# A graph network's attention sweep: node work cut into pieces between groups, two node one-hot buffers, no filling matmuls

## The chip, the core and the metric

The program runs on one core of one Trainium2 chip, as one launch. The metric is the device time of that launch in microseconds. The engines are named as the profile names them: PE (TensorE; PEld is its weight load), DVE (VectorE), ACT (ScalarE), POOL (GpSimd) and SP (SyncE). Each runs its own list of instructions in order, and they wait for each other through semaphores.

## The reference

Four graph layers, each added to its input and normalised over the 64 features, over 12,500 nodes and 200,000 edges (sorted by destination). The change touches only the first, an attention layer with four heads:

```python
h = (x @ W).reshape(N, H, D)
a_src = jnp.einsum('nhd,hd->nh', h, att_src)
a_dst = jnp.einsum('nhd,hd->nh', h, att_dst)
alpha = leaky_relu(a_src[src] + a_dst[dst], 0.2)
alpha = jnp.exp(alpha - amax[dst])
denom = segment_sum(alpha, dst)
msg = h[src] * (alpha / denom[dst])[:, :, None]
out = segment_sum(msg, dst).reshape(N, H * D) + bias
x = layernorm(x + out @ Wl + bl)
```

## The kernel before

Seven passes go over the graph: `gat` (this layer), then `dev`, `gine` and four `sage` passes. The change is in `gat`, which takes about microseconds 180 to 2990 of the profile; then a table of edge counts is built and the other passes use it.

**Tiling.** The 200,000 edges, ordered by destination, are cut into 392 groups of 512 (4 columns of 128). The 12,500 nodes are 98 tiles of 128, and 7 tiles are a block, so there are 14 blocks. Destinations are skewed: the first block takes 14 rounds of 8 groups (112 groups), the last a single round. A group whose edges end in one tile and begin in the next has a further tile ("second tile" in the code) and needs its one-hot and its sum twice.

**One group.** SP loads the edges' indices and a copy of their destinations. POOL gathers the sources' rows with four indirect DMAs (L671) into one of 8 slots, so it can be up to some groups ahead. DVE makes a node one-hot (L1683, nodes by edges, for each tile of the group), and PE multiplies it with the nodes' scores (`expand`, 12 narrow matmuls of L879 per tile, opened by L872 and closed by L883), which gives every edge its destination's score. DVE adds the scores (L1701 to L1706, `logit_ready`), ACT takes the exponent (L1127) and issues the load of the edges' features (L1130, `edges_loaded`), and then makes the one-hot of edges by nodes (L1135, L1138). DVE multiplies rows by weights (L1712, `messages_ready`), PE sums messages per node (`aggregate`: L833 narrow, then L844, 8 wide f32 matmuls), and DVE adds the sum to the block's accumulator (L1650). A further tile's one-hot is L1644 on DVE.

**Order.** The code is written out by hand. PE does `expand(g + 1)` ahead of `aggregate(g)`; DVE makes the node one-hot of group g + 1 inside group g. There is one buffer `nodehot`, so the second one-hot of a group waits (`expand_done`) until PE has read the first. Ahead of `logit_ready`, ahead of every `nodehot_ready` and ahead of `messages_ready`, PE multiplies zeros with zeros (`fill`, L817): 5, 5 per tile, and 6 matmuls of 128 columns.

**End of a block.** DVE normalises the block's sums (`gat_normalise`, L1294, L1439 to L1447), PE transposes them (`node_tensor`, L729, 14 matmuls), ACT copies the transposed sums to SBUF (L1212). Their product with the folded output weights (`gat_product`, L770, 28 matmuls), the residual sum, the layer norm (L1346 to L1326, with a square root on ACT, L1166) and the cutting into three bf16 parts (L1294, L1355, L1333 on DVE; L1183 and three DMAs on ACT) are the late half. It is done one block later, ahead of that block's own transposes: `late_half`, with `b - 1`. At the end of the last block both late halves remain, one ahead of its transposes and one behind them:

```python
def dense(b, late=None):       # PE
    if late:
        late()                 # gat_product(b - 1)
    node_tensor(pe, k, b)
    pe.wait_ge(step_sem["copied"], ...)
```

PE enters the next block's rounds only when the copy has ended.

## Time and profile before

| what | us |
|---|---|
| median of 3 runs | 10120.04 |
| lowest and highest | 10109.03 and 10133.09 |
| span of the profiled execution | 10126.3 |
| PE, DVE, POOL and ACT busy in it | 6982.7, 4777.3, 4577.3, 1864.3 |

The page gives the profiled execution's span, and no separate time of that execution; the span is within 6.3 us of the median of the runs. The busy shares (69%, 47%, 45%, 18%) are over seven passes with different limits, so they say little on `gat`. The stretch to read is that of the sweep, cut at the ends of blocks: a block ends where ACT copies (L1212), and the first instruction of each group on DVE is L1701. The timeline's "idle before" names what ended the wait; "issue" means nothing that the profile shows.

### The profile page before, as it was taken

What the parts mean: (1) busy time and instruction counts of PE and PEld (TensorE: products, weight loads), DVE (VectorE), ACT (ScalarE), POOL (GpSimd) and SP (SyncE); (2) the same over time, 40 slices, a digit from 0 to 9 for tenths busy, and PEclk for the clock granted to TensorE, in tenths of its full rate; (3) what the DMA queues carried; (4) which work ended last, traced back from release to release, by engine and by line L of the source; (5) the groups of instructions that cost most, each with busy time, mean ns of one, the idle gap of its engine ahead of it and who ended that gap; (6) DMA issues with size and microseconds to landing.
All of it is one profiled execution on the core that took longest, in us unless ns stands there. A gap on an engine that the chain in (4) does not pass through costs nothing.

```text
span 10126.3 us, 269255 instructions
## 1 busy us (share of the span) xinstructions
PE 6982.7 (69%) x70494; PEld 5130.6 (51%) x70495; DVE 4777.3 (47%) x12912; ACT 1864.3 (18%) x3800; POOL 4577.3 (45%) x4467
## 2 busy tenths in 40 slices
PE   5888777787754666666777876675777455565677
PEld 4666656565541222112454545665676454454676
DVE  4555555554458877776444333333332332333344
ACT  2333333332220234553000000000000000000000
POOL 3777665554420000001763017442653765763764
PEclk9898888888877888999888987887888677777788
DMA  2444333333320112234555566665676677677676
GB/s 64 95 95 91 88 83 89 83 79 74 72 69 13 63 78 111 127 128 167 164 174 183 177 211 194 213 213 184 215 237 213 201 275 265 207 254 240 205 261 233
DMA packets 973408, 1566.58 MB, mean 155 GB/s; under 512 B 499841, under 2 KB 621441, under 8 KB 966402
## 3 DMA queue, kind: packets, MB, share of 16 engines
q1 hardware_dynamic: 485762, 1244.14, 35.5%
q0 software_dynamic: 150016, 196.43, 9.4%
q10 hardware_dynamic: 337280, 122.87, 4.7%
q14 instruction: 317, 2.60, 0.1%
q8 instruction: 33, 0.54, 0.0%
HBM read 1337.91 MB, written 225.00 MB: 154 GB/s over the span
## 4 chain that ended last, share of the span: by engine, by line
PE 36%; issue 21%; DVE 16%; DVEq 11%; POOL 10%; DMA 5%; ACT 1%; ACTq 0%; SPq 0%; POOLq 0%
PE ps_turn L997 15%; POOL ARENA L671 10%; PE ps_out L844 6%; PE ps_turn L952 4%; PE ps_pair L844 2%; DMA ARENA<-edge_attr 2%; DVE ARENA L1834 2%; DVE ARENA L1836 2%; PE ps_turn L817 2%; DMA ARENA<-counts 2%; DVEq L1841 1%; PE ps_pair L1019 1%; DVEq L466 1%; PE ps_pair L879 1%; DVE ARENA L1924 1%
## 5 line engine op out<-in xcount | busy, mean ns | idle before, releaser
L997 PE MATMUL ps_turn<-ARENA 128*128 128x192 bf16 (+2 forms) x28812 | 2789.3, 266 | 760.6 <-DVE DSUM L1987 347.0
L997 PEld LDWEIGHTS ps_turn<-ARENA 128*128 128x128 bf16 x28812 | 2353.9, 108 | 1206.1 <-issue 901.0
L671 POOL DMA_INDIRECT ARENA<-table_sage,idx x1920 | 1876.0, 977 | 1330.9 <-issue 985.7
L671 POOL DMA_INDIRECT ARENA<-table_gat,idx x1568 | 1740.9, 1110 | 1044.4 <-DMA idx<-src_r 537.1
L952 PE MATMUL ps_turn<-ARENA 128*128 128x392 bf16 (+1 forms) x4204 | 1064.6, 359 | 673.7 <-DVE ARENA L1836 376.5
L671 POOL DMA_INDIRECT ARENA<-table_dev,idx x480 | 473.2, 986 | 1665.2 <-ACT idx L1220 1520.6
L1834 DVE TENSOR_SCALAR ARENA<-ARENA 128x784 bf16<-128x784 f16 (+1 forms) x2102 | 1008.6, 480 | 358.4 <-issue 229.0
L952 PEld LDWEIGHTS ps_turn<-ARENA 128*128 128x128 bf16 (+1 forms) x4204 | 334.3, 101 | 1403.7 <-issue 1359.6
L671 POOL DMA_INDIRECT ARENA<-table_gine,idx x480 | 468.4, 976 | 908.0 <-issue 687.5
L1202 ACT ACTIVATE ARENA<-ps_turn 128x784 f32 x784 | 645.3, 823 | 1081.7 <-PE ps_turn L952 1080.9
L1987 DVE TENSOR_REDUCE DSUM<-ps_turn 128x64 f32<-128x192 f32 (+2 forms) x686 | 263.6, 384 | 1137.5 <-PE ps_turn L997 975.5
L817 PE MATMUL ps_turn<-ZEROS 128*128 128x128 bf16 x6762 | 571.3, 226 | 239.7 <-issue 185.3
L1914 DVE SCALAR_TENSOR_TENSOR ARENA<-DST,TBASE,COL 128x512 f32 x720 | 493.6, 747 | 512.8 <-issue 512.8
L817 PEld LDWEIGHTS ps_turn<-ZEROS 128*128 128x128 bf16 x6762 | 436.6, 101 | 375.0 <-issue 338.1
L1019 PE MATMUL ps_pair<-ARENA 128*128 128x64 bf16 (+2 forms) x8640 | 388.2, 209 | 313.2 <-DMA ARENA<-table_sage,idx 161.4
L844 PE MATMUL ps_out<-ARENA 128*128 128x320 f32 x1568 | 565.6, 513 | 0.0
L1220 ACT ACTIVATE idx<-ARENA 128x16 int32 x192 | 40.7, 215 | 2778.6 <-PE ps_turn L1041 2693.4
L1135 ACT ACTIVATE tmp<-COL,dst_in 128x128 bf16<-128x128 f32 x1568 | 501.1, 390 | 253.7 <-issue 253.7
L1019 PEld LDWEIGHTS ps_pair<-ARENA 128*128 128x128 bf16 x8640 | 363.6, 108 | 335.7 <-issue 333.0
L1836 DVE TENSOR_SCALAR ARENA<-ARENA 128x128 bf16<-128x128 f16 (+1 forms) x2102 | 521.3, 248 | 0.0
L844 PE MATMUL ps_pair<-ARENA 128*128 128x320 f32 x1568 | 509.0, 471 | 0.0
L1034 PE MATMUL ps_out<-ARENA,more_hots 128*128 128x64 bf16 (+2 forms) x3528 | 227.4, 216 | 388.5 <-issue 217.6
(303 smaller groups left out, 6737.4 us busy)
## 6 DMA issues: line engine op xcount, KB each, us to landing
ARENA<-counts SPq DMA_DIRECT2D x1764, 448.0 KB
counts<-ARENA SPq DMA_DIRECT2D x49, 3136.0 KB, 9.0
ARENA<-counts SPq DMA_DIRECT2D x588, 224.0 KB
ARENA<-dst_b SPq DMA_DIRECT2D x393, 256.0 KB
ARENA<-edge_attr ACTq DMA_DIRECT2D x392, 128.0 KB
ARENA<-table_sage,idx POOLq DMA_INDIRECT x1920
ARENA<-table_gat,idx POOLq DMA_INDIRECT x1568
nodes_dev<-table_rows ACTq DMA_DIRECT2D x14, 672.0 KB
```

The costliest lines, as they stand in the source:

```text
L671: pool.indirect_dma_start(ps["buf"][:, s, c, 0:ps["row"]], None, ps["table"][:, :], bass.IndirectOffsetOnAxis(idx[:, s, c:c + 1], 0)).then ...
L817: pe.matmul(ps_fill, ZERO[:, :], ZERO[:, :], start=True, stop=True)
L844: last = pe.matmul(sums[:, 0:MSGW if gat else n], lhs, rhs, start=(c == 0 and q == 0), stop=(c == C - 1 and q == parts - 1))
L952: last = pe.matmul(ps_turn[:, at:at + WIDE_ROW // 2], marks[:, 0:P], marks[:, P + q * (WIDE_ROW // 2):P + (q + 1) * (WIDE_ROW // 2)], star ...
L997: last = pe.matmul(ps_dense[half][:, 0:n], RING[:, b, :], XP[:, b, :], start=(b == PIECE_AT[pieces[0]]), stop=(j == pieces[-1] and b == PI ...
L1019: last = pe.matmul(ps_pair[:, (4 * h + q) * P:(4 * h + q) * P + n], tile_hots[:, ((4 * h + q) * C + c) * P:((4 * h + q) * C + c + 1) * P], ...
L1135: act.activation(distance[:, c * P:(c + 1) * P], COL[:, :], ACT.Abs, scale=-1.0, bias=dst_in[:, s % 2, c:c + 1]).then_inc(hot_distance, 1)
L1202: act.activation(to[:, :, c * CHUNK:(c + 1) * CHUNK].rearrange("p (q b) v -> p q b v", q=2), sums.rearrange("p q (b v) -> p q b v", v=CHUN ...
L1834: ve.tensor_scalar(marks[:, P:P + WIDE_ROW], IOTA16, BASES[:, bass.ds(q, 1)], KEY_pad[:, bass.ds(j, 1)], ALU.add, ALU.is_equal).then_inc(r ...
L1836: ve.tensor_scalar(marks[:, 0:P], COL16, AKEY_pad[:, bass.ds(j, 1)], None, ALU.is_equal).then_inc(ready, 1)
L1914: return ve.scalar_tensor_tensor(ring.rearrange("p (c v) -> p c v", c=C), DST[:, bass.ds(cols, C)].unsqueeze(2).broadcast_to([P, C, P]), T ...
L1987: ve.tensor_reduce(DSUM[:, half, 0:n], ps_dense[half][:, 0:3 * n].rearrange("p (q v) -> p v q", q=3), X_AXIS, ALU.add).then_inc(dense_read, 1)
```

## The change

Four things are changed, all in `gat`.

1. The late half of block b is cut into pieces, and the pieces stand between the groups of the first round of block b + 1: `gat_product` on PE in `expand` of group slot 2, the head (residual sum, mean, variance) on DVE behind slot 3, the square root on ACT behind slot 4, the tail (scale, cut) on DVE behind slot 5, the rows' copies and DMAs on ACT behind slot 7. A phase register per engine says whether a piece is due; every round tests it, and a round that has none due branches past it. A second copy of each piece stands ahead of `gat_normalise`, for a block that has no round.
2. `nodehots` has two buffers, and `expand_done` starts at 2.
3. The filling matmuls of zeros are gone.
4. At a block's end PE waits only for the copy of the last 256 columns (`end_copied`), which now comes first; the load of the old rows is issued behind the copies, into `big`.

```diff
-        nodehot = gat_area(GE // 2, dt=BF16)
+        nodehots = gat_area(GE, dt=BF16)
...
-        old_x = gat_area(TB * D).rearrange("p (t d) -> p t d", t=TB)
...
+        old_x = big[:, 0:TB * D].rearrange("p (t d) -> p t d", t=TB)
...
-        def sweep(eng, one_round, finish, dense, late=None):
+        def sweep(eng, phase, one_round, finish, dense, pieces):
+            eng.reg_mov(phase[0], NO_PHASE)
+            eng.reg_mov(phase[2], 0)
             with eng.Fori(0, BLOCKS) as b:
                 r0 = eng.value_load(SCHED[0:1, bass.ds(b, 1)], min_val=0, max_val=ROUNDS)
                 r1 = eng.value_load(SCHED[0:1, bass.ds(b + 1, 1)], min_val=0, max_val=ROUNDS)
@@ -504,16 +504,19 @@
                 last_block = eng.value_load(SCHED[0:1, BLOCKS + 1:BLOCKS + 2], min_val=0, max_val=BLOCKS)
                 with eng.If(last_block.eq(b)):
                     finish()
-                if late is None:
-                    dense(b)
-                else:
-                    dense(b, lambda: late_half(eng, b, late))
-            if late is not None:
-                late(BLOCKS - 1)
-        def late_half(eng, b, late):
-            with eng.If(b > 0):
-                late(nc.s_assert_within(b - 1, 0, BLOCKS - 1, skip_runtime_bounds_check_because="b > 0"))
+                for j, piece in enumerate(pieces):
+                    piece_here(eng, phase, j, piece)
+                dense(b)
+                eng.reg_mov(phase[0], 0)
+                eng.reg_mov(phase[2], b)
+            for piece in pieces:
+                piece(BLOCKS - 1)
+        def piece_here(eng, phase, j, piece):
+            with at_phase(eng, phase, j):
+                piece(eng.snap(phase[2], min_val=0, max_val=BLOCKS - 1))
+                eng.reg_add(phase[0], phase[0], 1)
...
-            def fill(n):
-                for _ in range(n):
-                    pe.matmul(ps_fill, ZERO[:, :], ZERO[:, :], start=True, stop=True)
...
-                def expand(g, lo, hi):
-                    fill(5)
+                def expand(g, lo, hi, product=False):
                     pe.wait_ge(logit_ready, g + 1)
+                    if product:
+                        settle(pe)
+                        piece_here(pe, gat_phase, 0, lambda b: gat_product(pe, b))
                     pe.matmul(ps_exp_all[:, 0:C * 2 * H], ZERO[:, :], ZERO[:, 0:C * 2 * H], start=True, stop=False)
                     with pe.Fori(lo, hi) as t:
                         pe.reg_add(spread, spread, 1)
-                        fill(5)
                         pe.wait_ge(nodehot_ready, pe.snap(spread, min_val=1, max_val=GROUPS * TILES))
+                        hot = nodehots[:, bass.ds(pe.snap(spread_at, min_val=0, max_val=GE), GE)]
                         for c in range(C):
                             for q in range(3):
-                                last = pe.matmul(ps_exp[:, c, :], nodehot[:, c * P:(c + 1) * P],
+                                last = pe.matmul(ps_exp[:, c, :], hot[:, c * P:(c + 1) * P],
                                                  VALS[:, bass.ds(t, 1), q, :].rearrange("p a k -> p (a k)"),
                                                  start=False, stop=False)
                         last.then_inc(expand_done, 1)
+                        pe.reg_alu(spread_at, spread_at, GE, ALU.bitwise_xor)
...
-                            expand(g + 1, *next_span(pe, spans, s))
+                            expand(g + 1, *next_span(pe, spans, s), s == 2)
...
-                            fill(6)
...
-                def dense(b, late=None):
-                    if late:
-                        late()
+                def dense(b):
                     node_tensor(pe, k, b)
-                    if gat:
-                        pe.wait_ge(step_sem["copied"], block_count("copied", "gat", b))
-                        settle(pe)
+                    pe.wait_ge(end_copied, b + 1)
+                    settle(pe)
...
+                    if s == 4:
+                        piece_here(act, gat_phase, 0, lambda b: node_root(0, b, b))
+                    if s == 7:
+                        piece_here(act, gat_phase, 1, lambda b: node_rows(0, b, b))
...
-            def gat_copy(b, late):
-                late()
+            def gat_copy(b):
                 act.wait_ge(step_sem["turned"], block_count("turned", "gat", b))
                 act.wait_ge(product_read, b + 1)
                 settle(act)
+                act.activation(bigT[:, 1536:TB * H * D], ps_turn[:, 1536:TB * H * D], ACT.Copy).then_inc(end_copied, 1)
+                act.activation(bigT[:, 0:1536], ps_turn[:, 0:1536], ACT.Copy).then_inc(step_sem["copied"], 1)
                 act.dma_start(old_x, x.rearrange("(t p) d -> p t d", p=P)[:, bass.ds(b * TB, TB), :]).then_inc(old_x_loaded, 16)
-                act.activation(bigT[:, :], ps_turn[:, 0:TB * H * D], ACT.Copy).then_inc(step_sem["copied"], 1)
...
-                xb = a[:, :, 0:D]
-                ve.wait_ge(step_sem["product"], block_count("product", ps["name"], b))
-                ve.wait_ge(old_x_loaded, b * 16 + 16)
-                step(ve.tensor_tensor(y, view(ps_gat, D), old_x, ALU.add))
-                ve.sem_inc(product_read, 1)
-                step(ve.tensor_tensor(y, y, row(CV[:, :]), ALU.add))
-                layer_norm(b, y, xb)
-                both = view(big, 2 * D)
-                if not isinstance(b, int):
-                    ve.wait_ge(step_sem["turned"], block_count("turned", "gat", b) + 1)
-                    settle(ve)
-                step(same(both[:, :, 0:D], xb))
-                step(ve.tensor_tensor(both[:, :, D:2 * D], xb, xb, ALU.mult))
-                store_parts(2 * D)
+                xb, y = a[:, :, 0:D], view(tmp[:, 2, :], D)
+                if head:
+                    ve.wait_ge(step_sem["product"], block_count("product", ps["name"], b))
+                    ve.wait_ge(old_x_loaded, b * 16 + 16)
+                    step(ve.tensor_tensor(y, view(ps_gat, D), old_x, ALU.add))
+                    ve.sem_inc(product_read, 1)
+                    step(ve.tensor_tensor(y, y, row(CV[:, :]), ALU.add))
+                    centre(b, y)
+                if tail:
+                    scale(b, y, xb)
+                    both = view(big, 2 * D)
+                    step(same(both[:, :, 0:D], xb))
+                    step(ve.tensor_tensor(both[:, :, D:2 * D], xb, xb, ALU.mult))
+                    store_parts(2 * D)
...
-            ve.wait_ge(rows_free, b + 1)
+            ve.wait_ge(rows_free, b + 2)
...
+                        if s == 3:
+                            ve.wait_ge(expand_open, g + 2)
+                            settle(ve)
+                            piece_here(ve, gat_phase, 0, lambda b: late(b, True))
+                        if s == 5:
+                            piece_here(ve, gat_phase, 1, lambda b: late(b, False))
```

How the instruction lists move. TensorE, slot 1 of a round, the expansion of the next group. Before:

```order
L817 MATMUL ps_turn<-ZEROS 128x128 x5
L871 REGISTER_ALU
L872 MATMUL ps_pair<-ZEROS 128x32 [waits logit_ready]
L873 UNCONDITIONAL_BRANCH
L873 ISA
L817 MATMUL ps_turn<-ZEROS 128x128 x5
L879 ISA [waits nodehot_ready]
L879 MATMUL ps_pair<-ARENA 128x8
L879 ISA
L879 MATMUL ps_pair<-ARENA 128x8
L879 ISA
L879 MATMUL ps_pair<-ARENA 128x8 x10
```

TensorE, the same place in the changed kernel:

```order
L873 MATMUL ps_pair<-ZEROS 128x32 [waits logit_ready]
L874 UNCONDITIONAL_BRANCH
L874 ISA
L877 ISA [waits nodehot_ready]
L880 ISA
L880 MATMUL ps_pair<-ARENA 128x8
L880 ISA
L880 MATMUL ps_pair<-ARENA 128x8
L880 ISA
L880 MATMUL ps_pair<-ARENA 128x8
L880 ISA
L880 MATMUL ps_pair<-ARENA 128x8 x3
```

The zeros (`ps_turn<-ZEROS`) are gone, and because the one-hot's address is now in a register, more register instructions (`ISA`) stand between the narrow matmuls.

ScalarE, from the one-hot of slot 4 to the exponent of slot 5. Before:

```order
L1138 ACTIVATE ARENA<-tmp,ONE 128x512 [waits hot_distance]
L1126 REGISTER_ALU
L1127 ACTIVATE ARENA<-ARENA 128x4x4 [waits logit_ready]
L1130 ISA
L1130 DMA ARENA<-edge_attr 128x4x64
```

ScalarE, the same place in the changed kernel:

```order
L1136 ACTIVATE ARENA<-tmp,ONE 128x512 [waits hot_distance]
L457 REGISTER_ALU
L458 COMPARE_AND_BRANCH
L518 ISA
L1166 ACT_TABLE_LOAD
L1166 ACTIVATE small<-small 128x7 [waits var_ready]
L519 REGISTER_ALU
L517 UNCONDITIONAL_BRANCH
L1124 REGISTER_ALU
L1125 ACT_TABLE_LOAD
L1125 ACTIVATE ARENA<-ARENA 128x4x4 [waits logit_ready]
```

The square root with its table load is branched past where it isn't due, but the second table load, ahead of the exponent, stands outside the branch and is done in every round.

VectorE, the beginning of the late half's head. Before, behind the normalising of a block's sums (`big<-ARENA,small`):

```order
L1447 TENSOR_TENSOR big<-ARENA,small 128x1792
L78 REGISTER_ALU
L515 COMPARE_AND_BRANCH [waits vector_step]
L1345 ISA [waits product]
L1346 TENSOR_TENSOR tmp<-ps_pair,ARENA 128x448 [waits old_x_loaded]
L78 ISA
L1348 TENSOR_TENSOR tmp<-tmp,CV 128x448 [waits vector_late_step]
```

VectorE in the changed kernel, behind slot 3 of a round (`L1742` is the last of that slot):

```order
L1742 REGISTER_ALU
L457 REGISTER_ALU [waits expand_open]
L458 COMPARE_AND_BRANCH
L518 ISA
L1364 ISA [waits product]
L1365 TENSOR_TENSOR tmp<-ps_pair,big 128x448 [waits old_x_loaded]
L78 ISA
L1367 TENSOR_TENSOR tmp<-tmp,CV 128x448 [waits vector_late_step]
```

The head now stands between two groups, behind a wait for the next group's expansion that every round makes.

## Rows read from the trace of the kernel before

**Rows 1.** Stretches; per engine busy us (x instructions), then TensorE's granted clock, DMA share.
```profile
...
core 0: us, PE busy (x) PEld busy (x) DVE busy (x) ACT busy (x) POOL busy (x), PEclk, DMA share, GB/s
190.00:827.00 637.00, 539.98 (x5848) 404.19 (x5847) 339.73 (x1024) 248.89 (x667) 499.85 (x451) 0.90 0.43 95
...
827.00:2980.00 2153.00, 1664.44 (x17822) 1257.43 (x17822) 1093.01 (x3059) 712.68 (x1772) 1204.85 (x1104) 0.87 0.36 81
...
```

**Rows 2.** Waits of POOL from 180 to 827: releaser, total us, times, longest us.
```profile
...
POOL ARENA L671 <- issue: 137.5, 451, 0.3
...
```

**Rows 3.** Waits of POOL from 827 to 2980.
```profile
...
POOL ARENA L671 <- DMA idx<-src_r: 536.2, 119, 32.9
...
```

**Rows 4.** The stretch 827 to 2980, line 1701 alone (one instruction per group).
```profile
...
827.00:2980.00 2153.00, 48.10 (x280) 0.87 0.36 81
...
```

**Rows 5.** The stretch 827 to 2980, line 1644 alone (one per further tile).
```profile
...
827.00:2980.00 2153.00, 66.89 (x89) 0.87 0.36 81
...
```

**Rows 6.** Timeline, end of block 0: start us, duration us, engine, work, idle before.
```profile
...
810.30 0.17 DVE L1701 TENSOR_TENSOR ARENA<-ps_pair,ARENA 128x16 f32<-128x16 f32 x1
...
828.26 0.17 DVE L1701 TENSOR_TENSOR ARENA<-ps_pair,ARENA 128x16 f32<-128x16 f32 x1 [7.91 <-issue]
...
```

**Rows 7.** Timeline, end of block 1, DVE, PE and ACT.
```profile
...
1055.94 0.17 DVE L1701 TENSOR_TENSOR ARENA<-ps_pair,ARENA 128x16 f32<-128x16 f32 x1 [0.39 <-PE ps_pair L883]
...
1066.37 3.38 PE L770 MATMUL ps_pair<-MST,bigT 128*128 128x64 f32 x28
...
1069.89 0.62 DVE L1346 TENSOR_TENSOR tmp<-ps_pair,ARENA 128x448 f32<-128x448 f32 x1 [2.31 <-PE ps_pair L770]
...
1078.16 1.09 DVE L1333 TENSOR_TENSOR tmp<-big 128x896 f32<-128x896 f32 x1
...
1085.40 1.28 ACT L1212 ACT_TABLE_LOAD   x1 [2.54 <-issue]
...
1088.95 0.17 DVE L1701 TENSOR_TENSOR ARENA<-ps_pair,ARENA 128x16 f32<-128x16 f32 x1 [9.71 <-issue]
...
```

**Rows 8.** Timeline, end of block 12.
```profile
...
2869.88 0.17 DVE L1701 TENSOR_TENSOR ARENA<-ps_pair,ARENA 128x16 f32<-128x16 f32 x1 [0.92 <-DVE ARENA L1650]
...
2898.96 0.17 DVE L1701 TENSOR_TENSOR ARENA<-ps_pair,ARENA 128x16 f32<-128x16 f32 x1 [9.65 <-issue]
...
```

**Rows 9.** Waits of DVE from 827 to 2980.
```profile
...
DVE ARENA L1683 <- PE ps_pair L879: 259.7, 84, 7.3
...
```

**Rows 10.** Timeline, a group with one tile behind another.
```profile
...
1047.69 0.17 DVE L1701 TENSOR_TENSOR ARENA<-ps_pair,ARENA 128x16 f32<-128x16 f32 x1 [0.91 <-PE ps_pair L883]
...
1052.19 0.45 PE L833 MATMUL ps_pair<-ARENA 128*128 128x5 bf16 x12 [0.74 <-DMA ARENA<-edge_attr]
...
1052.49 2.40 PE L844 MATMUL ps_pair<-ARENA 128*128 128x320 f32 x8
...
1054.73 0.44 PE L817 MATMUL ps_turn<-ZEROS 128*128 128x128 bf16 x5
...
1055.31 0.45 PE L879 MATMUL ps_pair<-ARENA 128*128 x12
...
1056.41 0.45 PE L833 MATMUL ps_out<-ARENA 128*128 128x5 bf16 x12 [0.26 <-issue]
...
```

**Rows 11.** Timeline, a node one-hot pair between two sums.
```profile
...
2514.43 2.40 PE L844 MATMUL ps_out<-ARENA,tmp 128*128 128x320 f32 x8
...
2517.84 0.49 DVE L1683 TENSOR_SCALAR ARENA<-ARENA,NODE 128x512 bf16<-128x512 int32 x1 [7.00 <-PE ps_pair L879]
...
2518.48 0.65 PE L879 MATMUL ps_pair<-ARENA 128*128 x12 [0.48 <-DVE ARENA L1683]
...
2519.93 0.44 PE L833 MATMUL ps_pair<-ARENA 128*128 128x5 bf16 x12
...
```

**Rows 12.** Timeline, one group's sum some microseconds earlier.
```profile
...
2510.20 4.09 PE L844 MATMUL ps_out<-ARENA 128*128 128x320 f32 x8
...
```

**Rows 13.** Waits of ACT from 827 to 2980.
```profile
...
ACT ARENA L1127 <- DVE ARENA L1706: 987.9, 278, 15.3
...
```

More of the change, by code:

```diff
@@ L1313, in layer_norm, with centre @@
             def layer_norm(b, y, dst):
-                mean, var, std = small[:, 0, 0:TB], small[:, 1, 0:TB], small[:, 2, 0:TB]
+                centre(b, y)
+                scale(b, y, dst)
+            def centre(b, y):
+                mean, var = small[:, 0, 0:TB], small[:, 1, 0:TB]
                 sq = view(tmp[:, 3, :], D)
```

58 lines of the change are left out of this document (34 added, 24 removed).

## The prediction

> **What bounds the kernel now.** I read the page's slices first, then the same counts cut at the ends of blocks, then the waits of POOL, DVE and ACT in the two stretches that this shows, and then the timelines of one group, one pair of one-hots and one block's end. The sweep has two regimes. Up to 827 us (block 0, 112 groups) POOL is the bound: its gathers are busy for 499.85 of 637 us [rows 1], and between them it only pays its own issue time, 137.5 us over 451 gathers, with no wait for a slot worth naming [rows 2]. A gather costs 1.4 us there, so a group 5.6 us, whatever PE and DVE do. From 827 to 2980 us (blocks 1 to 13) POOL is busy for 1204.85 of 2153 us [rows 1] and waits 536.2 us for indices [rows 3], whose load waits for a free slot: the consumers, PE, DVE and ACT, are the bound. That stretch holds 280 groups [rows 4] in 35 rounds, and 89 further tiles [rows 5], so 369 sums on PE. Only there can the change win. What POOL would need for the 1104 gathers at block 0's price is 1104 x 1.4 = 1546 us, so up to 607 us of the stretch are open, and POOL doesn't cut the forecast below. What comes behind the sweep is the same code and is left at its time.
>
> **Term 1, the ends of blocks.** The end of block 0 has no late half in it: from the last group's first DVE instruction to the next block's it takes 828.26 - 810.30 = 18.0 us [rows 6]. The end of block 1 has one and takes 1088.95 - 1055.94 = 33.0 us [rows 7]; the twelfth after it, of block 12, takes 2898.96 - 2869.88 = 29.1 us [rows 8]. I take the mean of these two of twelve, 31.1. The difference of 13.1 us is DVE's half (1069.89 to 1079.25), PE's product of 3.38 us ahead of the transposes, and ACT's copies behind them [rows 7]. It leaves the end. At 18 us the end is set by DVE's way into the next block (7.9 us of idle behind the normalising, [rows 6]), so the copy's order (256 columns first) gives nothing more; the table load of 1.28 us [rows 7] now starts only when the transposes are done, but still ends in that cover. DVE, PE and ACT gain two branches each: I take 0.5 us. 13 x (13.1 - 0.5) = 164 us less, the thirteenth being the one behind the last block, of the same kind.
>
> **Term 2, the same work between groups.** It isn't gone. PE's 3.4 us go between two groups; DVE's head (five instructions of 0.62 us, some small ones) is 4.4 us, its tail 4.6 us. The wait for `expand_open` at slot 3 queues nothing that would not have waited for it at slot 4. Behind the head on DVE stands the next group's L1701, and PE waits for it with the expansion after next; meanwhile PE has one sum of 2.40 us [rows 10] to do. Bounds: 0, if the slack of PE and DVE takes it all, and 3.4 + 4.4 + 4.6 = 12.4 us, if none. PE is nearly full in this stretch (1664.44 of 2153 us, [rows 1]), so I take no cover for its part, and about 40% for DVE's: 8.5 us. 13 x 8.5 = 110 us more. ACT's part (square root, three copies, DMAs) stands behind slots 4 and 7; ACT waits 987.9 us for 278 exponents in this stretch [rows 13], 3.6 us each, and slot 7 is followed by DVE's own way round the loop: nothing.
>
> **Term 3, the second one-hot.** With one buffer DVE stands 259.7 us in 84 waits for PE to read the first one-hot [rows 9]. PE pays too: in [rows 11] its sum ends at 2516.83 and the next begins at 2519.93, a gap of 3.10 us. In it are 21 filling matmuls and 0.48 us of waiting for the second one-hot. In the group with one tile the gap is 1056.41 - 1054.89 = 1.52 us [rows 10]. With two buffers DVE makes both one-hots and the messages long before PE has finished its sum; what stays is two expansions of 0.45 us, opening and closing, about 1.1 us. So PE gains 2.0 us of a gap of 3.1; DVE's 259.7 / 84 = 3.1 us is the other end. I take 2.3: 89 x 2.3 = 205 us less (bounds 1.0, the fills of one such gap alone, and 3.1).
>
> **Term 4, the fills in groups with one tile.** Five fills show as 0.44 us [rows 10]; the 16 hold PE, pipelined, for about 1.1 of the 1.52 us. But the group has another chain: from L1701 (1047.69) over the exponent and the load of the edges' features to the sum that waits for that load (1052.19) it is 4.50 us [rows 10]. L1701 of group g + 1 waits for an expansion that PE does behind the sum of g - 1, so two groups cost at least 4.50 + 2.7 (the sum) + 0.9 (the expansion) = 8.1 us, 4.05 each. The group of [rows 10] takes 1056.41 - 1052.19 = 4.22 us. The gain is then 0.17 there, more where PE runs at half clock and the fills cost double. Bounds 0 and 1.1; I take 0.35, near the row: 191 x 0.35 = 67 us less. In block 0 it gives nothing, POOL covers it.
>
> **Term 5, the clock.** The granted clock is 0.87 in the stretch [rows 1]; with its two levels of 1.2 and 2.4 GHz that is 26% of the time at 1.2. A sum takes 2.40 us at the upper [rows 10] and 4.09 at the lower [rows 12], 1.7 more. The fills are part of what keeps PE busy, and DVE, PE and the edge load now leave gaps in their place, so the clock must fall somewhat. Against a collapse speaks rows 11 and 12 together: the sum at 2510.20 ran at the lower clock, was itself 4.09 us of unbroken matmuls, and the sum at 2514.43 was back at 2.40. A slow sum fills PE and brings the clock back. I take a clock of 0.80, 40% at the lower level: 369 x 0.14 x 1.7 = 88 us more. Bounds: 0, and all at the lower level, 369 x 0.74 x 1.7 = 464.
>
> The Trainium skill, "TensorE: Matmul & The Clock Gate", section "Part 1: The HAM clock gate (the "warmup" mystery)", says that the engine is throttled by default and that activity releases the throttle, and its table "Why this matters for your kernels" asks to keep TensorE busy. That speaks against this edit. The trace agrees on the direction (rows 11 and 12); if the rule were followed to its end the sum would be that of rival B.
>
> **Term 6, small things in every round.** Three engines test the phase and branch; ACT loads a table of 1.28 us [rows 7] ahead of slot 5's exponent, mostly inside its 3.6 us of waiting [rows 13]. 0.7 us x 35 = 25 us more (bounds 0 and 2). The register instructions between the narrow matmuls: the 12 matmuls of a first tile take 0.45 us and those of the second, with two such instructions visible, 0.65 [rows 10, 11]; six more would be 0.6 us where PE has just been released, and nothing where its sequencer is ahead during a sum. 0.1 x 369 = 37 us more (bounds 0 and 0.6 each, 220).
>
> **Sum.** -164 + 110 - 205 - 67 + 88 + 25 + 37 = -176 us. The profiled span was 10126.3, which gives 9950. That span is 6 us above the median of the runs, less than I can resolve, so 9950 is the forecast for the median as well.
>
> **Rivals.**
> A: the moved work is hidden and the clock holds. Terms 2 and 5 near zero: 10126 - 176 - 110 - 88 = 9750. For it: DVE is busy for only 1093 of 2153 us [rows 1], and POOL shows that the slots are full at the ends. Against it: the chain of a group passes DVE four times, so its idle time isn't free time, and PE has 23% left.
> B: slower, by the clock. Without fills PE stays at 1.2 GHz for most of the sweep. Terms as above with 464 in place of 88: 10126 - 176 + 376 = 10326; block 0 would add some, since a group at that clock takes 4.09 + 0.45 + about 1.1 = 5.6 us, just POOL's 5.6. It decides from where term 5 eats the other terms' 264 us: 264 / (369 x 1.7) = 0.42 more of the time, 68% at the lower level, a mean clock of 0.66. For it: the fills are 16 of a group's matmul instructions of full width, and there are gaps of idle at every block's end. Against it: rows 11 and 12.
> C: the work only changes its place. The pieces cost their full 12.4 us (term 2: 161), the one-hot pair gives 1.0 (term 3: 89): 10126 - 164 + 161 - 89 - 67 + 88 + 25 + 37 = 10117, no change. For it: nothing of the late half is removed. Against it: 259.7 us of DVE's waits have one cause that is removed.
>
> **How the numbers follow.** The forecast's own case, 9850 to 10040, has 66%; A 12%; C, with times from 10040 to 10146, 12%; B 10%. About 0.2%, 20 us, is what a measurement of this kernel tells from no change. Of C, half is faster by more than that. Faster: 0.66 + 0.12 + 0.05 = 0.83; the same 0.06; slower 0.11. The range 9820 to 10100 holds the forecast's case, half of A and half of C, and leaves B out.
>
> **What would show it.** Right: in the windows of block 0 no change and POOL still without waits for slots; DVE's waits for its node one-hot gone; ends of blocks of 18 to 19 us; the pieces' instructions in the first round of each block, with that round 8 us longer; a granted clock of about 0.80 in blocks 1 to 13; L833 waiting more often for the edges' load; POOL's waits for indices down from 536 to some 360 us. Wrong: a clock under 0.66 (B); rounds with pieces over 12 us longer (C); block 0 longer than 640 us, which would mean that PE at the lower clock has become slower than POOL.

## The result: 10060.1 us, 0.6% faster; the forecast was 9950

The changed kernel takes 10060.12 us (median of 4 runs, 10058.58 to 10074.73), the kernel before 10123.38 in the same session (4 runs). The ratio is 0.9938, 95% interval 0.9921 to 0.9955: 63 us less, where 173 were forecast. The profiled span went from 10126.3 to 10057.1 us.

I cut both traces by the start of the first VectorE instruction of every group (L1701 before, L1722 after; there are 392). The rows of this table are sums of such differences; "later pass" runs from the 181st to the 321st reduction of a step sum, in code that the change doesn't touch.

| us of the profiled execution | before | after | difference |
|---|---|---|---|
| block 0, 112 groups | 625.1 | 630.8 | +5.7 |
| its end | 18.0 | 19.1 | +1.1 |
| ends of blocks 1 to 12 | 375.5 | 229.2 | -146.3 |
| first round (8 groups) of blocks 1 to 12 | 668.5 | 820.3 | +151.8 |
| their other 22 rounds | 1026.7 | 1004.6 | -22.1 |
| block 13 | 53.4 | 60.8 | +7.4 |
| from its last group to the build | 52.0 | 40.9 | -11.1 |
| the later pass | 1322.4 | 1269.6 | -52.8 |
| all the rest | 5984.6 | 5981.7 | -2.9 |

So the sweep, which was to give everything, gave about 14 us, and 53 came from a pass with the same code as before. The ends of blocks are as forecast. The first rounds took back more than the ends gave.

The windows of the changed kernel, cut as those of [rows 1]; the columns are busy us by engine with instruction counts, then PE's clock:

```profile
182.00:831.00 649.00, 494.85 (x4058) 338.05 (x4058) 342.07 (x1037) 269.17 (x689) 504.17 (x465) 0.82 0.45 95
831.00:2974.00 2143.00, 1560.99 (x12930) 1095.77 (x12930) 1109.58 (x3065) 759.02 (x1820) 1189.49 (x1093) 0.79 0.36 81
```

The clock fell from 0.87 to 0.79, as term 5 had it (0.80). The waits of POOL, DVE and PE in the second of these windows (what waited, for what, us in total, times, longest):

```profile
POOL ARENA L674 <- DMA idx<-src_r: 538.5, 147, 16.3
...
DVE ARENA L1722 <- issue: 340.3, 122, 8.3
DVE ARENA L1669 <- PE ps_out L843: 303.5, 165, 3.3
DVE ARENA L1702 <- issue: 147.3, 246, 0.8
DVE ARENA L1722 <- PE ps_pair L885: 71.9, 62, 3.7
...
PE ps_out L832 <- DVE tmp L1663: 130.1, 26, 8.1
PE ps_pair L873 <- DVE ARENA L1727: 124.7, 36, 6.7
```

POOL waits for indices as long as in [rows 3], 538.5 against 536.2 us, so the consumers are not faster. DVE's 259.7 us of [rows 9], waiting for the node one-hot, are gone; L1669, the addition of a group's sums, now waits 303.5 us for PE (168.0 before, in the window of [rows 9]). ACT waits 1044 us for DVE to finish the scores it takes the exponent of, 988 in [rows 13].

One piece, in the first round of block 4 (start us, duration, what, and in brackets the idle time before it):

```profile
1563.16 0.48 DVE L1669 TENSOR_TENSOR ARENA<-ARENA,ps_out 128x325 f32 x1
1564.82 0.62 DVE L1365 TENSOR_TENSOR tmp<-ps_pair,big 128x448 f32<-128x448 f32 x1 [1.18 <-PE ps_pair L885]
1565.13 2.40 PE L843 MATMUL ps_pair<-ARENA 128*128 128x320 f32 x8
...
1565.59 0.62 DVE L1367 TENSOR_TENSOR tmp<-tmp,CV 128x448 f32<-128x448 f32 x1
...
1569.08 0.17 DVE L1337 TENSOR_SCALAR small<-small 128x7 f32<-128x7 f32 x1
...
1570.89 0.17 DVE L1722 TENSOR_TENSOR ARENA<-ps_pair,ARENA 128x16 f32<-128x16 f32 x1 [1.64 <-issue]
```

The head takes 1564.82 to 1569.25. PE's sum is over at 1567.5, 3.4 us before the next group's scores (L1722) can begin. PE has no work in between: the piece is the chain. It also waits 1.18 us for the expansion, whose last matmul began at 1564.04; PE had done the product from 1555.54 to 1558.85 and had no pause over 0.7 us from there on. That the product is what made the expansion late is likely by this, not shown. Behind the head, 1.07 of DVE's 1.64 us of idle time are the load of the next groups' spans into registers, which stands at slots 0 and 4 of every round.

### The profile page after: what moved, and what is told of

Same layout as the page of the kernel before. It is cut to its first block, busy times and chain, and to the rows that moved or that the text cites. A ratio compares the mean times of both kernels' runs of the same rounds, so it can differ in the third digit from the quotient of the medians.

```text
span 10057.1 us, 259505 instructions
## 1 busy us (share of the span) xinstructions
PE 6810.5 (68%) x63732; PEld 4878.1 (49%) x63733; DVE 4790.5 (48%) x12912; ACT 1926.9 (19%) x3863; POOL 4569.1 (45%) x4467
## 4 chain that ended last, share of the span: by engine, by line
PE 34%; issue 21%; DVE 18%; DVEq 12%; POOL 7%; DMA 7%; ACT 1%; SPq 0%; ACTq 0%; POOLq 0%
PE ps_turn L994 14%; PE ps_out L843 8%; POOL ARENA L674 7%; DMA ARENA<-edge_attr 4%; PE ps_turn L949 3%; DVE ARENA L1859 3%; DVE ARENA L1861 2%; DMA ARENA<-counts 2%; PE ps_pair L843 2%; DVEq L425 1%; PE ps_pair L1016 1%; DVEq L466 1%; DVEq L1859 1%; PE ps_out L832 1%; PE ps_out L1031 1%
## 5 line engine op out<-in xcount | busy, mean ns | idle before, releaser
L843 PE MATMUL ps_out<-ARENA 128*128 128x320 f32 x1568 | 677.2, 594 | 0.0
L843 PE MATMUL ps_pair<-ARENA 128*128 128x320 f32 x1568 | 556.7, 505 | 0.0
L1939 DVE SCALAR_TENSOR_TENSOR more_hots<-DST,TBASE,COL 128x512 f32 x294 | 221.2, 752 | 580.3 <-issue 580.3
L1733 DVE TENSOR_TENSOR ARENA<-ARENA 128x1024 f32<-128x1024 f32 x392 | 477.4, 1218 | 0.0
```

The source lines that it names most:

```text
L843: last = pe.matmul(sums[:, 0:MSGW if gat else n], lhs, rhs, start=(c == 0 and q == 0), stop=(c == C - 1 and q == parts - 1))
L1733: ve.tensor_tensor(msg[:, s % 2, :, 0:H * D].rearrange("p c (h d) -> p c h d", h=H), buf[:, s, :, 0:D].unsqueeze(2).broadcast_to([P, C, H, ...
L1939: return ve.scalar_tensor_tensor(ring.rearrange("p (c v) -> p c v", c=C), DST[:, bass.ds(cols, C)].unsqueeze(2).broadcast_to([P, C, P]), T ...
```

## Experiments on the forecast's terms

Each kernel ran in 5 rounds beside the kernel before; the ratios are to it, with 95% intervals. "First rounds", "ends" and "slots" (the interval from one group to the next, by the group's number in its round) are from starts of the same VectorE instruction as in the table above. A difference of two ratios is uncertain by about 0.2%, 20 us; a difference of two profiled spans is of one execution each.

**Zero matmuls alone.** The kernel before with an empty `fill`:

```diff
-                for _ in range(n):
-                    pe.matmul(ps_fill, ZERO[:, :], ZERO[:, :], start=True, stop=True)
+                return
```

> The kernel before without its zero matmuls (5 ahead of the scores wait, 5 per expanded tile, 6 ahead of the messages), nothing else changed. Theory S (the terms as forecast, each standing alone): T4 gives 67 us back and T5, the lower clock, costs 88, so +21: about 10145 us, mean granted clock of blocks 1 to 12 down from 0.87 to about 0.80. Rival R (the zero matmuls lie wholly in waits and only the clock matters): +40 to +90, 10165 to 10215, at the same clock. Rival N (neither reaches the end, since the first engine of the chain is VectorE or GpSimd): within 15 us of before. The stretch behind the sweep is the same code, so it should take the same 7129 us in each.

10185.91 us, 1.0058 (1.0045 to 1.0072), +59. Clock 0.81 in all, 0.82 in block 0 (0.90 before). In the profile the sweep is 26 us longer, of which 9 in block 0; that execution, at 10162 us, was the fastest of the five, 34 us longer than before's, and 9 of these lie in stages with the same code. The later pass is as slow as before. The median lies in the range of rival R, the profiled sweep near theory S (+21): this pair can't decide whether the zero matmuls cost anything where they stand.

**Two one-hots alone.** In the kernel before, with the pair in `more_hots`, used alternately by PE and DVE through `spread_at`:

```diff
-ve.tensor_scalar(nodehot[:, :], dstb[:, s % 2, :], ...)
+ve.tensor_scalar(nodehots[:, bass.ds(ve.snap(spread_at, min_val=0, max_val=GE), GE)], dstb[:, s % 2, :], ...)
+ve.reg_alu(spread_at, spread_at, GE, ALU.bitwise_xor)
```

> The kernel before with two node one-hots used in turn (in a buffer that only later passes use), with its zero matmuls and its long block ends. Theory S: T3 as forecast, 2.3 us in each of 89 further tiles, -205: about 9920 us. Rival R (behind the wait for the node one-hot stands another one that ends as late, TensorE's 12 matmuls or the sums of the group ahead): -60 at most, 10060 or more, and VectorE's wait at the end of the expansion or for the sums grows by most of the 260 us that leave the one-hot. Rival L: the 47 us that the later pass with unchanged code lost came from this edit; then they show here behind the sweep.

10053.26 us, 0.9926 (0.9911 to 0.9940). That is rival R for the sweep, and rival L: the later pass is 37 us shorter here too, so the edit to the sweep gave about 38 by the ratios, and 16 in the profiled sweep. In its trace PE's branch back to the head of the block loop takes 3.7 us, 13 times, where it took 0.2, 45 us in all; more on this below. With these taken off, the profiled sweep would be 61 us shorter.

**Two one-hots and no zero matmuls**, the two diffs above together, with the block ends of before:

> The kernel before with two node one-hots and no zero matmuls, long block ends as before. Parts as measured so far, adding up: -75 (two one-hots) +59 (no zero matmuls) -45 (the branch back of TensorE's shorter block loop is quick again) and no second gain from VectorE's shifted code: about 10070 us. Theory S (as forecast: -205 -67 +88 = -184): 9950. Rival W (with both, VectorE's wait moves wholly to the sums at the lower clock): 10110 or more.

10009.49 us, 0.9882 (0.9867 to 0.9897). I had expected 10070; S's 9950 was as far off on the other side. It beats the changed kernel by 51 us (57 by the ratios, 48 by the profiled spans), and differs from it by the late work and the copy's order only, and by where the one-hots lie. Against the first experiment, which has one one-hot and is else the same, the sweep is 79 us shorter: 22 in first rounds, 42 in the others, 4 in each of block 0 and the ends, 6 in block 13. Where the rest of 205 went shows in DVE's waits from 831 to 2950 us, first with one buffer, then with two:

```profile
DVE ARENA L1700 <- issue: 347.0, 150, 9.7
DVE ARENA L1682 <- PE ps_pair L878: 215.6, 81, 7.6
...
DVE ARENA L1649 <- PE ps_out L843: 194.0, 105, 5.1
...
DVE ARENA L1649 <- PE ps_pair L843: 33.7, 29, 2.5
```

```profile
DVE ARENA L1704 <- issue: 303.9, 108, 9.8
DVE ARENA L1652 <- PE ps_out L843: 280.0, 154, 5.8
...
DVE ARENA L1704 <- PE ps_pair L884: 60.3, 68, 2.7
DVE ARENA L1652 <- PE ps_pair L843: 51.6, 34, 2.4
```

215.6 us of waiting for the one-hot's reader go; the wait for PE's sums grows by 86 + 18 and that for the expansion's end to 60.3. I sorted the intervals from a group to the next by tiles, outside the first rounds of blocks 1 to 12 and without the ways back of the round loop. Where the groups on both sides of the interval's own have two tiles (18 times) it fell from 10.40 to 8.25 us, 2.15, about what was forecast for each; where only the next has two (32 times) from 5.82 to 5.35. The other 111 stayed as they were.

**The late work alone**, the changed kernel with one one-hot and its zero matmuls back (5, 5 and 6, as before):

```diff
-                        hot = nodehots[:, bass.ds(pe.snap(spread_at, min_val=0, max_val=GE), GE)]
+                        hot = nodehots[:, 0:GE]
+                            fill(6)
                             pe.wait_ge(messages_ready, g * 2 + 2)
```

> The changed kernel with one node one-hot and the zero matmuls back: only the late work in pieces and the short block ends are left of the change. Theory S: -164 (T1) +110 (T2) +62 (T6) = +8 on 10123: about 10130 us. Rival R (two one-hots and the missing zero matmuls together did next to nothing, pieces cost what they cost in the changed kernel, 152 us): the time of the changed kernel, 10060 us within 20. Rival I (the three parts help one another: a second one-hot only pays where pieces stand): above 10160 us. If the 47 us of the later pass show here too, they belong to the pieces or to the place of the data, not to the one-hots.

10212.58 us, 1.0082 (1.0067 to 1.0096). The ends are 155 us shorter and the first rounds 233 longer; 44 us of PE's slow branch are in it, and the later pass is 52 shorter. The profiled sweep is 129 us longer, without the slow branch 85. So the late work in pieces by itself makes the kernel slower, as only rival I had it, and more so than with two one-hots: there the sweep is 51 us longer without zero matmuls (10009 to 10060 us) and 44 with them (two one-hots alone against the next kernel, both with the slow branch).

**The changed kernel with its zero matmuls back:**

```diff
+                    fill(5)
                     pe.wait_ge(logit_ready, g + 1)
+                        fill(5)
                         pe.wait_ge(nodehot_ready, ...)
+                            fill(6)
                             pe.wait_ge(messages_ready, g * 2 + 2)
```

> The changed kernel with the zero matmuls back (5, 5 per tile, 6 as before). Theory S: 88 us of clock back, 67 us of single-tile groups lost again: about 10040 us, clock 0.87. Rival R (zero matmuls cost nothing, the clock does): 10060-88 = 9970 us. Rival N (at this state VectorE or GpSimd sets the rounds): 10045 to 10075 with the clock up all the same.

10098.68 us, 0.9969 (0.9957 to 0.9980), by the ratios 31 more than the changed kernel, with the clock at 0.90 in block 0. PE's slow branch is here again (13 times, 48 us in all, 45 more than the quick one). As it stands the time is above all three ranges. Without the slow branch this kernel would be some 7 (medians) to 16 us (profiled sweeps) faster than the changed one: that tells neither theory S (20 faster) nor rival N from no change, and only R (90 faster) is out.

**The changed kernel with one one-hot:**

```diff
-                        hot = nodehots[:, bass.ds(pe.snap(spread_at, min_val=0, max_val=GE), GE)]
+                        hot = nodehots[:, 0:GE]
```

> The changed kernel with one node one-hot in place of two. Theory M (two one-hots are worth what the pair without zero matmuls and without pieces shows, 78 us in the sweep, not the 205 forecast): 10135 to 10150 us. Rival I (pieces make it worth more, as in the pair with zero matmuls and pieces, 106 us): 10155 to 10175. Theory S (205): 10265.

10171.77 us, 1.0049 (1.0037 to 1.0062), 112 more: rival I. In kernels with pieces the second one-hot is worth 112 without and 114 with zero matmuls; in those without pieces it is worth 79 and 61 in the sweep; nowhere 205.

## Experiments on the price of a piece

**Five copies on DVE at slot 3 of each round**, added to the kernel with two one-hots, no zero matmuls and no pieces:

```diff
+                        if s == 3:
+                            for q in range(5):
+                                ve.tensor_copy(nodehot..., COL...).then_inc(extra, 1)
+                                ve.wait_ge(extra, i * 5 + (q + 1))
```

> The kernel with two one-hots, no zero matmuls and no pieces, plus 5 copies of 128x512 on VectorE, one after the other, at slot 3 of each round, into a buffer that nobody reads (it adds work and removes none). A copy is estimated at 0.5 us and its wait, so 2.5 to 3.3 us per round. Theory P (VectorE's time between groups lies on the path in full, the reason why pieces cost 14 us a block and not 8.5): 35 rounds of blocks 1 to 13 x 2.9 = 100 us more, 10110, and 0 to 10 more in block 0, which GpSimd sets. Theory S (40% is covered, as term 2 assumed): 60 us more, 10070. Rival Z (VectorE has slack, PE's and ACT's parts of the pieces cost): 20 us or less, up to 10030.

10173.77 us, 1.0054 (1.0041 to 1.0067), 164 more than without them (152 in the profiled sweep). The copies in one round:

```profile
1167.69 2.46 DVE L1725 CAST ARENA<-COL 128x512 bf16<-128x512 f32 x5
1171.70 0.17 DVE L1704 TENSOR_TENSOR ARENA<-ps_pair,ARENA 128x16 f32<-128x16 f32 x1 [1.54 <-issue]
```

2.46 us of work made a round of blocks 1 to 12 longer by 3.36 us on average (114 us in 34 rounds), and one of block 0 by 2.79 (39 us in 14). Theory P had 2.9 us and 10110 in all, and nearly nothing in block 0; the result is 60 us above it. DVE has no cover for this work at slot 3, though it is busy for half of the time, and not in block 0 either, which I had called POOL's: POOL there waits 39.4 us for indices, 3.1 without the copies. In the 22 other rounds slot 3 grew by 2.9 us, slot 5 by 1.0, and slot 4 shrank by 0.5, so the delay is seen again two groups later. Part of the excess is the clock, 0.79 in place of 0.82 in block 0 and of 0.80 behind it: an estimate from the two lengths of a sum, 2.40 and 4.09 us, gives 11 us in block 0 and 13 in blocks 1 to 13. The rest of the excess isn't explained.

**The wait for the expansion only where a piece is due:**

```diff
-                            ve.wait_ge(expand_open, g + 2)
-                            settle(ve)
-                            piece_here(ve, gat_phase, 0, lambda b: late(b, True))
+                            piece_here(ve, gat_phase, 0, lambda b: late(b, True, g))   # waits inside
```

> The changed kernel, but VectorE waits for the opened expansion (expand_open, slot 3) only where a piece is due, once in a block and not in every round. Theory W (this wait is what makes slot 3 of the rounds without a piece 0.8 to 1.0 us longer than in the kernels without pieces): 25 to 35 us less, 10025 to 10035. Rival N (VectorE would wait for it at slot 4 anyway, and the branch on the phase is what costs): within 10 us of the changed kernel, 10050 to 10070.

10054.05 us, 0.9929 (0.9916 to 0.9941), 6 less than the changed kernel and not to be told from it. Slot 3 of the other rounds fell from 7.1 to 6.6 us, slot 4 rose from 4.7 to 5.1: rival N, as far as the wait goes. What its branch costs wasn't measured.

**The pieces ahead of the addition of sums**, so that they run in DVE's wait for PE:

```diff
+                        if s == 3: ...        # the same lines as before, moved up
+                        if s == 5: ...
                         sum_last(s, g, *last_span(ve, spans, s))
-                        if s == 3: ...
-                        if s == 5: ...
```

> The changed kernel with VectorE's two pieces moved by a few instructions inside their slots: behind the group's messages and ahead of the addition of the last group's sums, instead of behind it. Theory G (a piece costs its full length since it stands behind the wait for TensorE's sum, 1.8 us each where there is one; ahead of it, that wait covers part of it): 13 blocks x 2 pieces x 1 to 1.7 us, 25 to 45 us less, 10015 to 10035. Rival H (TensorE then waits for the late addition or for the next group all the same): within 10 us, 10050 to 10070. Rival B (the sums' buffers come free later and TensorE loses more than VectorE gains): 10080 or more.

10073.42 us, 0.9952 (0.9938 to 0.9965), 13 more. DVE's wait for PE's sums fell from 303.5 to 258.7 us, and the time did not. First rounds gained 12 us, the others lost 20 (slot 3 rose from 7.1 to 8.1 us, where the wait for the expansion, in every round, now stands ahead of the addition). The time is 3 us above rival H's range; of G's 25 to 45 us nothing shows in sum.

**The last 6 zero matmuls of a group kept**, on the kernel with two one-hots and no pieces, on the changed kernel, and on the changed kernel with early pieces:

```diff
+                            fill(6)
                             pe.wait_ge(messages_ready, g * 2 + 2)
```

> The kernel with two one-hots, no pieces, and only the last 6 zero matmuls of a group kept (the 10 ahead of an expansion are gone). TensorE's block loop is still shorter than before's. Theory K (6 zero matmuls keep more of the clock than they cost, as they stand where TensorE waits for the messages anyway): clock 0.83 in the sweep, 15 to 35 us less than with none, 9975 to 9995. Rival N (what the clock gives the zero matmuls take): 10000 to 10020. Rival L (the branch back costs again at this place or length): 10050 or more.

> The changed kernel with the last 6 zero matmuls of a group back. Its TensorE block loop stays shorter than before's. Theory K (they are worth here what they were worth without pieces, 29 us, through the clock): 10025 to 10040 us. Rival N (with pieces TensorE has less left, nothing gained): 10050 to 10070. Rival L (the branch back to the head of the block loop becomes slow again, 13 x 3.7 us): 10080 or more.

> Both of the last two edits on the changed kernel: pieces ahead of the addition, and the last 6 zero matmuls of a group. If they add up, 25 to 45 and 20 to 30 us less than the changed kernel: 9985 to 10015 us. If pieces can't pay at all, it stays above the 9981 us of the kernel with two one-hots, 6 zero matmuls and no pieces. Rival H for the pieces: 10025 to 10040.

Without pieces 9980.65 us, 0.9861 (0.9847 to 0.9876), 29 less than with no zero matmuls (21 by the ratios). With pieces 10032.64, 0.9913 (0.9899 to 0.9926), 28 less (25). With early pieces 10042.54, 0.9924 (0.9910 to 0.9938), 31 less (28). One such difference is hardly above its uncertainty of 20; the three agree, theory K held for the first two, and the third lies 3 us above rival H's range. The first is the best kernel of this study: 139 us under the kernel before and 80 under the changed one. The windows from 183 and from 830 us, first without zero matmuls, then with the six:

```profile
183.00:815.00 632.00, 481.91 (x4007) 330.61 (x4008) 337.68 (x1024) 247.86 (x672) 495.61 (x448) 0.82 0.43 96
830.00:2960.00 2130.00, 1485.90 (x12930) 1057.08 (x12930) 1118.88 (x3078) 717.08 (x1776) 1185.71 (x1103) 0.80 0.36 84
```

```profile
183.00:815.00 632.00, 511.17 (x4720) 363.31 (x4721) 340.69 (x1033) 248.29 (x671) 493.95 (x453) 0.85 0.45 96
830.00:2960.00 2130.00, 1552.10 (x14591) 1133.11 (x14589) 1147.23 (x3094) 714.90 (x1770) 1192.36 (x1097) 0.82 0.37 83
```

## Experiments on the time that came from unchanged code

In the later pass DVE leaves a loop of six trips and starts the next unit with L1382. In the kernel before it stood still there. The two rows of DVE around the first of these places in the kernel before:

```profile
6161.04 0.22 DVE L1924 TENSOR_TENSOR ARENA<-ARENA,ps_out  x1 [1.70 <-issue]
6165.89 0.62 DVE L1382 TENSOR_TENSOR tmp<-Web,DEG 128x448 f32<-128x448 f32 x1 [4.62 <-issue]
```

In the trace's record of branches, DVE's branch at 6161.63 is followed by the next instruction, a register move with no wait, at 6164.67. Six such gaps at this branch take 32 us, and six more ahead of L1383 17 us, 49 together. The kernel without zero matmuls, whose DVE code lies at the same places, has them too (48 us), and so have the two below with instructions added on PE only; no kernel whose DVE code differs has.

**18 instructions more, no work moved.** The kernel before, with this between the sweep and the build on DVE:

```diff
+                for _ in range(18):
+                    settle(ve)      # a semaphore increment that nothing waits for
```

> The kernel before with 18 semaphore increments on VectorE, that nothing waits for, between the attention sweep and the build: they shift VectorE's later code by 18 instructions and move no work. Theory P (the 37 to 54 us that the later pass with unchanged code lost in four kernels come from where VectorE's code lies: at the end of that pass's unit loop its sequencer stood 6 times 5.4 us and 6 times 2.8 us before, and not in those four): that pass 35 to 55 us shorter, 10070 to 10095 us. Rival O (they come from something else in those kernels, such as the sweep's own state or the place of the data): within 10 us of before, 10122 to 10142.

10077.46 us, 0.9953 (0.9940 to 0.9967): 44 us faster, with no change to what is computed or when. The wait of L1382 in that pass (6050 to 7000 us), before, here, and of the same instruction in the changed kernel:

```profile
DVE tmp L1382 <- issue: 53.1, 12, 8.1
```

```profile
DVE tmp L1382 <- issue: 21.6, 12, 1.9
```

```profile
DVE tmp L1400 <- issue: 21.6, 12, 1.9
```

The later pass takes 1283.9 us, before 1322.4. An edit that makes DVE's earlier code longer can bring this. Ahead of these two instructions the changed kernel's DVE stands idle 48 us less than before's; so 40 to 50 of its 63 us have nothing to do with what it does.

**PE: 64 instructions that never run**, first inside the block loop, then ahead of it:

```diff
+                        with pe.If(pe.snap(never, min_val=0, max_val=1) > 0):
+                            fill(32)
```

> The kernel before with 32 zero matmuls behind a branch that is never taken, in TensorE's block loop behind the wait for the copy: 64 instructions longer, none of them run. Theory C (TensorE's branch back to the head of the block loop costs 3.7 us, 13 times, once the loop is longer than before's, as it did in three kernels that add code): +40 to +55 us, 10170 to 10190. Rival O (the 3.7 us came with the work that those kernels add): within 10 us of before.

> The same 64 instructions that never run, ahead of TensorE's block loop: the loop is as long as before's and lies 64 instructions later. If length decides, as theory C says, nothing changes: 10122 to 10142 us. Rival P (the place decides, not the length): 13 branches of 3.7 us here too, 10170 to 10190.

Inside: 10192.81 us, 1.0067 (1.0054 to 1.0081). Ahead: 10183.49, 1.0055 (1.0041 to 1.0068). My theory C was wrong on the second: with the loop as long as before's, 64 instructions later is enough. Place decides, at least here. The branch's own time is 62 us more inside and 48 ahead (13 branches, each case). PE's branches of the block loop, in the second kernel and in the changed one (min/median/max ns):

```profile
L498 PEldq COMPARE_BRANCH  x14: 77/3696/5058, 819.5 to 3020.3; - x14
```

```profile
L498 PEldq COMPARE_BRANCH  x14: 78/210/220, 829.4 to 2963.5; - x14
```

The page of the profile lists the queues that fetch instructions (packets, MB, share of the engines). Before, 18 instructions later on DVE, 64 later on PE, with two one-hots alone, and changed:

```profile
q14 instruction: 317, 2.60, 0.1%
q8 instruction: 33, 0.54, 0.0%
```

```profile
q14 instruction: 288, 2.36, 0.1%
q8 instruction: 33, 0.54, 0.0%
```

```profile
q8 instruction: 146, 2.39, 0.1%
q14 instruction: 317, 2.60, 0.1%
```

```profile
q8 instruction: 146, 2.39, 0.1%
q14 instruction: 288, 2.36, 0.1%
```

```profile
q14 instruction: 289, 2.37, 0.1%
q8 instruction: 28, 0.46, 0.0%
```

q8 goes from 33 to 146 (149 in one) in exactly the five kernels in which PE's branch is slow; in the others it has 28 to 35. That a fetch of code is what the branch waits for is inferred from this, no row names it. q14 falls from 317 to 288 with DVE's shift, but it is no full guide: it has 325 in the two kernels with pieces and one one-hot, whose later pass is as fast. The Trainium skill, "Runtime: NRT & Kernel Launch", section "Instruction fetch mechanics", says of a taken branch to code outside the engine's two pages that it "forces a DMA fetch of the target page before execution can continue", with pages of 16 KiB. The trace agrees in the size, 2.39 MB in 146 packets is 16.4 KB each, and in that 113 more packets go with 13 slow branches. These are nearly nine for a branch, more than the one page that the sentence speaks of.

## Why the forecast was wrong

10060 lies in the band of rival C, 10040 to 10146, and C's sign came up: first rounds are 12.6 us longer than before, where I had said 8, and over 12 for C. C's own sum, 10117, less the 53 us of the later pass is 10064. That it fits so well is luck in part, since its terms miss on both sides. It is luck too that the time lies in my range of 9820 to 10100: without the 48 us from where DVE's code lies it would be about 10108.

**Term 1 (-164): right.** The ends of blocks 1 to 12 fell from 31.3 to 19.1 us each, 146 us, and the one behind the last block by 11.

**Term 2 (+110): the overlap was wrong.** "About 40% for DVE's" cover had no row behind it, and there is none. Against the kernel that differs by the late work only, first rounds cost 168 us more in 12 blocks, 14.0 each, and block 13 17 more, 185 in place of 110, above even my upper bound of 12.4 a block, 161 in all. The slots say where: slot 3, with the head, went from 6.1 to 12.1 us; slot 5, with the tail, from 6.1 to 11.8; slot 2, with PE's product, +2.0; slot 7, with ACT's copies, which I had at nothing, +2.4; slot 0 gave 1.8 back. So it was DVE's part that had no cover: some 9 us of work cost 11.7, while PE's 3.3 cost 2.0 in its own slot. Rival A's own caution ("its idle time isn't free time") is what the five copies showed: 2.46 us of work cost 3.36. In sum the late work in pieces costs 51 us; by my terms 1, 2 and the 25 of 6 it was to give 29. That is rival C's mechanism, and a little over its price.

**Term 3 (-205): mis-sized, the largest miss.** It gave 79 us in the sweep without pieces and 112 in the kernel with them, both net of the register instructions that I had put at 37 in term 6. The 2.3 us hold in the 18 intervals with pairs on both sides (2.15); I gave them to all 89 further tiles. Behind the wait that goes there was another nearly as late, the one for PE's sums. C's 1.0 each, 89, was near. Nor do terms 2 and 3 add up, as my sum took for granted: with one one-hot the late work costs 85 us in the sweep, with two 44 to 51.

**Terms 4 and 5 (-67, +88): the sum near, the parts not parted.** In the profiled sweeps, with PE's slow branch taken off, going without the 16 costs 26 and 27 us in the two pairs with one one-hot and 8 and 16 us in those with two; the forecast was +21. (The medians of the first pair have +59, a part of it in stages with the same code.) With two one-hots, going from 16 to 6 gains 11 us with pieces and 22 without, so the ten ahead of the expansions do cost something; the last six give 28 to 31 us by the medians. The clock was forecast at 0.80 and found at 0.79. Block 0, which I had left out of both terms, lost 9 us, at a clock of 0.82 in place of 0.90.

**Term 6 (+25, +37):** between the kernels with and without pieces the other rounds differ by 11.5 us in 22, 0.5 each against 0.7. The register instructions on PE were not measured by themselves.

**Not on the list at all:** where code lies. It gave 40 to 50 us by DVE. On PE it took 44 to 62 us of branches from five of the test kernels, and by chance nothing from the changed one. Without it the changed kernel would be some 15 us faster than before, which its interval can't tell from no change.

The ledger by steps of the profiled spans: without zero matmuls +34.3; with two one-hots -151.6, of which 79 in the sweep and 48 in the later pass; with the late work in pieces +48.1; together -69.2, the measured difference. The other 25 of the second step lie in stages with the same code, which differ by up to 18 us each between kernels here. What stays open is the rule by which a place of PE's block loop is good or bad: length and place can't be parted by two kernels. Another experiment on term 2 that I would want, DVE's work made smaller in place of moved, wasn't tried.

## What to carry to other kernels

Idle time of an engine inside a loop that passes it four times a group was no slack here: before work is moved into it, add the same amount of dummy work there and time it. When a wait is removed, look for the one that ends next on the same engine, interval by interval; its average over all cases isn't its price. Before a gain of under 1% is put down to an edit in code with loops, compare the untouched stages and the instruction queues' packets, and time a kernel that only shifts the code.

## What the runs showed of the hardware

- 18 instructions that do nothing, on DVE, made the kernel 44 us faster; 64 that never run, on PE, made it 62 to 71 us slower. PE's slow branch of the block loop is 3.7 us at the median in four kernels, 4.9 in the fifth, and up to 5.7; the idle time behind DVE's in the later pass is up to 6.5.
- DVE stands still at every way back of the round loop, in all kernels: 2.7 to 3.3 us between the branch and the next instruction, with no wait, up to 5.3 in the kernels with pieces, 35 times in the sweep, 100 to 115 us in all. That it is of the same kind as the branches above isn't shown. With the load of the spans it makes the step to the next round's first group, in the kernel with two one-hots and no zero matmuls:

```profile
1137.64 0.48 DVE L1652 TENSOR_TENSOR ARENA<-ARENA,ps_out 128x325 f32 x1
1144.06 0.17 DVE L1704 TENSOR_TENSOR ARENA<-ps_pair,ARENA 128x16 f32<-128x16 f32 x1 [5.93 <-issue]
```

  That is why slot 7 takes 11 us where others take 5 to 6. No kernel here tried to shorten DVE's round loop; by the row it's the largest single idle time left in a round.
- Six zero matmuls ahead of a wait are worth 28 to 31 us of 10,000 by the medians (21 to 28 by the ratios); with them the clock goes from 0.80 to 0.82 in blocks 1 to 13 and from 0.82 to 0.85 in block 0, which is the likely way they act.
